# Two groups of narrow heads packed side by side before the output projections of a Flamingo-style stack

## The reference

```python
x = x + tanh(g_xattn[0]) * L0_xattn(layernorm(x), ctx)         # 16 heads of 64 over the context: "wide"
x = x + tanh(g_ffn[0])   * L0_ffn(layernorm(x))                # 16 heads of 16 over x, then 8 routed experts
x = x + tanh(g_xattn[1]) * L1_xattn(ctx, ctx, layernorm(x), mask, w_out, b_out)  # 16 heads of 16 over the context, masked
x = x + tanh(g_ffn[1])   * L1_ffn(layernorm(x))                # 16 heads of 16 over x, plus a dense mixture of 8 experts
```

## Time and profile before

| | |
|---|---|
| median of 3 runs | 3478.32 us (3477.23 to 3482.04) |
| profiled execution, its own time | 3479.19 us |
| its span, first to last instruction | 3477.0 us |
| TensorE busy | 3308.9 us (95%) |
| VectorE busy | 2020.1 us (58%) |
| ScalarE busy | 1439.3 us (41%) |
| GpSimd busy | 957.2 us (28%) |
| mean granted TensorE clock | 0.978 of full speed |

### The profile page before, as it was taken

How to read it: one execution, slowest core, us unless ns; L and a number is a source line. 1 busy time by engine, 2 the same in 40 slices (tenths; PEclk the granted TensorE clock), 3 DMA queues, 4 the chain that set the end, 5 groups by cost and what they waited for, 6 DMA issues and landing times.

```text
span 3477.0 us, 45530 instructions
## 1 busy us (share of the span) xinstructions
PE 3308.9 (95%) x18530; PEld 1442.0 (41%) x18530; DVE 2020.1 (58%) x4314; ACT 1439.3 (41%) x1645; POOL 957.2 (28%) x469
## 2 busy tenths in 40 slices
PE   7999999999999999999997979998999999999999
PEld 4444444444444445434442752223323343333354
DVE  4444445554665465565565027776767677666546
ACT  3443434444334443344433212454454435544434
POOL 4665555454465553554500000110000000000000
PEclk9999999999999999999999999999999999999999
DMA  4000000000000000000021430211111111110000
GB/s 154 11 13 13 32 8 11 13 7 32 8 19 11 13 26 8 25 10 8 4 97 49 125 108 18 60 39 49 35 35 36 35 29 25 51 35 26 13 19 13
DMA packets 68252, 114.94 MB, mean 33 GB/s; under 512 B 4849, under 2 KB 49545, under 8 KB 67530
## 3 DMA queue, kind: packets, MB, share of 16 engines
q1 hardware_dynamic: 62666, 97.08, 8.8%
q0 software_dynamic: 5376, 14.95, 1.9%
HBM read 101.79 MB, written 16.78 MB: 34 GB/s over the span
## 4 chain that ended last, share of the span: by engine, by line
PE 85%; DVE 7%; ACT 4%; POOL 2%; DMA 1%; issue 1%; ACTq 0%; DVEq 0%; POOLq 0%
PE ring L1266 10%; PE pv L1160 10%; PE ring L1149 9%; PE pv L1287 9%; PE ring L1227 3%; PE ring L1259 3%; PE ring L1121 3%; PE ring L1130 3%; PE ring L1122 3%; PE ring L1146 3%; PE ring L1107 3%; PE ring L1272 2%; PE ring L1108 2%; ACT wide L1435 2%; PE ring L1345 2%; PE ring L1326 2%
## 5 line engine op out<-in xcount | busy, mean ns | idle before, releaser
L1532 POOL TENSOR_TENSOR wide<-wide 124x1024 f32<-124x1024 f32 (+1 forms) x341 | 804.2, 2358 | 263.9 <-ACT wide L1428 227.7
L1435 ACT ACTIVATE wide<-ring 124x1024 f32<-124x1024 f32 (+2 forms) x544 | 528.5, 1022 | 549.4 <-PE ring L1266 547.0
L1651 DVE TENSOR_REDUCE max_a<-ring 128x2 f32<-128x802 f32 x512 | 491.9, 991 | 373.0 <-PE ring L1130 372.8
L1428 ACT ACTIVATE wide<-ring 124x1024 f32<-124x1024 f32 (+1 forms) x416 | 425.6, 1027 | 445.5 <-PE ring L1149 404.3
L1679 DVE CUSTOM_DVE_ANT_0 rest<-ring,slim 128x401 bf16<-128x401 f32 x683 | 374.3, 577 | 138.1 <-PE ring L1227 134.2
L1149 PE MATMUL ring<-wide 64*124 64x512 f32 (+1 forms) x1664 | 428.6, 593 | 0.0
L1160 PE MATMUL pv<-wide 124*64 124x512 f32 (+1 forms) x1664 | 413.0, 611 | 3.5 <-ACT wide L1428 3.5
L1689 DVE TENSOR_REDUCE slim<-ring 128x2 f32<-128x1024 f32 x256 | 307.5, 1221 | 111.6 <-PE ring L1239 110.3
L1266 PE MATMUL ring<-slim 32*128 32x512 f32 x2176 | 351.1, 646 | 3.0 <-DVE max_b L1679 2.3
L1502 POOL DMA_DIRECT2D slim<-in_ctx_k x16 | 8.8, 549 | 992.8 <-PE ring L1227 628.6
L1529 POOL TENSOR_TENSOR wide<-wide 124x1024 f32<-124x1024 f32 x31 | 73.4, 2369 | 557.9 <-ACT wide L1428 435.7
(11 more groups left out here) (239 smaller groups left out, 4096.2 us busy)
## 6 DMA issues: line engine op xcount, KB each, us to landing
slim<-in_ctx_k SPq DMA_DIRECT2D x16, 800.5 KB, 4.3
wide<-in_w_pair SPq DMA_DIRECT2D x32, 384.0 KB, 3.1
slim<-in_ctx_v SPq DMA_DIRECT2D x16, 744.0 KB
wide<-in_w SPq DMA_DIRECT2D x16, 512.0 KB, 4.8
wide<-in_we SPq DMA_DIRECT2D x16, 512.0 KB, 3.7
wide<-in_ctxT SPq DMA_DIRECT2D x4, 1601.0 KB, 6.6
slim<-in_ctx_k POOLq DMA_DIRECT2D x16, 400.2 KB, 4.7
wide<-padded_x SPq DMA_DIRECT2D x8, 640.0 KB, 4.8
```

The lines of the kernel that those rows point to most:

```text
L1428: sc.activation(exps_a[0:kn, slot_of[unit], :], slot[0:kn, :], ACT.Exp, scale=WIDE ** -0.5).then_inc(scalar_done, 1)
L1435: sc.activation((exps_2 if blk == 2 else exps_34)[0:kn, first + 2 * i:first + 2 * i + 2, :].rearrange("p h n -> p (h n)"), ring_t[0:kn, ba ...
L1532: po.tensor_tensor(sums[0:kn, :], sums[0:kn, :], view, ALU.add).then_inc(pool_done, 1)
L1651: ve.reduce_max(max_a[:, :, q, c], slot.rearrange("p (h n) -> p h n", h=2)[:, :, 0:CHUNK], AX.X).then_inc(vector_done, 1)
```

## The change

The host now packs the projection weights without padding: `ow` and `w_out` come as two tiles of 128 full rows instead of four with 64 zero rows. Rows 32h to 32h+15 of tile i belong to head h of group 2i, and rows 32h+16 to 32h+31 to head h of group 2i+1. In `tailb` the product of VectorE no longer goes back into `rest` but into one half of each block of 32 columns in a tile that two groups share (the upper half of `outT`). The transpose back is done once for two groups, behind the second. `outb` has two matmuls instead of four for each 128 tokens; in block 4 these have 128 columns each instead of 64. The wait for `outT` to be free stands ahead of the product instead of the transpose. `scatter` grows by 64 columns. The order strings are other ones, with the new costs, and the first `kproj` of a batch is kept behind the last `vproj` of the batch before.

```diff
-C_BASE = C_SCATTER + GROUP * SLIM
+C_BASE = C_SCATTER + P
...
+    def side_by_side(w, places):
+        out = w[places].reshape(GROUPS // 2, 2, GROUP, SLIM, w.shape[-1]).transpose(0, 2, 1, 3, 4)
+        return np.ascontiguousarray(out.reshape(GROUPS // 2, P, w.shape[-1]).transpose(1, 0, 2))
...
-        "ow": padded(a("L0_ffn_ow"), KV_MAJOR), "w_out": padded(a("L1_xattn_w_out").T, HEAD_MAJOR),
+        "ow": side_by_side(a("L0_ffn_ow"), KV_MAJOR), "w_out": side_by_side(a("L1_xattn_w_out").T, HEAD_MAJOR),
...
-    "33333332333333333333333233330030331103033113003130311130003113003111332233334300031333113003033113030331113000"
+    "33333332333333333333333233330030331130011330033130311130003113003111333233432300303310331113000313331130003113"
...
+    if unit[0] == "tailb":
+        v = 4 if unit[3] % 2 else 3
...
+                held = (("vproj", b - 1, PAIRS - 1, 1),) if b and p == 0 else ()
...
-            yield Step(0.88, (("sc", 0.6), ("ve", 2.3)) if last else (), 0, (("scoreb", blk, b, g, k),) + valued + also,
+            yield Step(0.88, (("sc", 0.6), ("ve", 2.25 if g % 2 else 1.55)) if last else (), 0, (("scoreb", blk, b, g, k),) + valued + also,
...
-        yield Step(7.0 if blk != 4 else 4.4, (("ve", 2.5),), 1,
+        yield Step(3.5 if blk != 4 else 2.2, (("ve", 2.5),), 1,
...
-                        for g in range(GROUPS):
+                        for i in range(GROUPS // 2):
                             if blk == 4:
-                                c0 = q * D + g * GROUP * SLIM
-                                last = pe.matmul(slot[:, c0:c0 + GROUP * SLIM], outT_b[blk][:, g, q * P:(q + 1) * P], scatter,
-                                                 start=True, stop=True)
+                                last = pe.matmul(slot[:, q * D + i * P:q * D + (i + 1) * P], outT_b[blk][:, i, q * P:(q + 1) * P],
+                                                 scatter, start=True, stop=True)
                             else:
-                                last = pe.matmul(slot[:, q * D:(q + 1) * D], outT_b[blk][:, g, q * P:(q + 1) * P],
-                                                 (w_out2 if blk == 2 else w_out3)[:, g, :], start=g == 0, stop=g == GROUPS - 1)
+                                last = pe.matmul(slot[:, q * D:(q + 1) * D], outT_b[blk][:, i, q * P:(q + 1) * P],
+                                                 (w_out2 if blk == 2 else w_out3)[:, i, :], start=i == 0, stop=i == GROUPS // 2 - 1)
...
-                    ve.tensor_tensor(blocks(rest)[:, :, 0:SLIM], blocks(rest)[:, :, 0:SLIM],
+                    for lane, other in plan.tile_free[unit]:
+                        past.wait_ge(*at(lane, *other))
+                    two, side = outT_b[blk][:, GROUPS // 2 + g // 2, :], SLIM * (g % 2)
+                    ve.tensor_tensor(blocks(two)[:, :, side:side + SLIM], blocks(rest)[:, :, 0:SLIM],
                                      inverse[:, :].unsqueeze(2).to_broadcast([P, S // 32, SLIM]), ALU.mult).then_inc(vector_done, 1)
-                    after(n + 3)
-                    for lane, other in plan.tile_free[unit]:
-                        past.wait_ge(*at(lane, *other))
-                    ve.transpose(outT_b[blk][:, g, :], rest[:, :]).then_inc(vector_done, 1)
+                    if g % 2:
+                        after(n + 3)
+                        ve.transpose(outT_b[blk][:, g // 2, :], two).then_inc(vector_done, 1)
```

More of the change, by code:

```diff
@@ L82, in lay_out @@
         consts[HEAD_MAJOR[g] % P, C_STRIP + g * P + STRIP] = 1
-    consts[STRIP - 1, C_SCATTER + np.arange(GROUP * SLIM)] = 1
+    consts[:, C_SCATTER:C_BASE] = np.eye(P).reshape(2, GROUP, SLIM, P).transpose(1, 0, 2, 3).reshape(P, P)
     consts[:, C_BASE:C_SPARE] = CAPACITY * np.arange(EXPERTS)
@@ L145 @@
[L145 to L149, removed]
@@ L158 @@
+    "111744745575755555555555555656575565576557557656575657565755765657565576575766767677777777"
 )
 TURNS_3 = (
[L162 to L165 removed]
@@ L171 @@
[L171 to L174 removed]
+    "00333333333333333333333333333333333333333331333133231303231332332011323323112013233231333231333233133331332332"
@@ L175 @@
+    "32231333254171462452171421241421421254624146521712561652175622674644746444747444474455464546454644467445546454"
+    "6454644467445546454464546447476575656576676"
 )
@@ L382, in wide_prep @@
                 for c in range(2):
-                    yield Step(2.75, (("sc", 0.9), ("ve", 0.6)), 1, gate, ("kproj", b, p, c))
+                    yield Step(2.75, (("sc", 0.9), ("ve", 0.6)), 1, gate + held, ("kproj", b, p, c))
                     emit(on(in_slot(("kproj", b, p, c), "scalar"), *k_free[s], *free["kB"]))
@@ L766, in flamingo @@
         wide = sb("wide", [P, 20736])
-        slim = sb("slim", [P, 19361])
+        slim = sb("slim", [P, 18849])
         consts = sb("consts", [P, C_ALL])
@@ L869, in flamingo @@
         gqa_w = part(slim, 12032, FT, (GROUPS + 1) * P + KV_HEADS * SLIM)
-        w_out2 = part(slim, 13440, GROUPS, D)
+        w_out2 = part(slim, 13440, GROUPS // 2, D)
         xn_a = part(slim, 14464, QT, D)
@@ L880, in flamingo @@
         kq_3b = half(slim, 14210, CTX + 1 + S)
-        w_out3 = part(slim, 15488, GROUPS, D)
-        xnT_3 = part(slim, 16512, FT, S)
-        low_b = half(slim, 18560, CTX)
+        w_out3 = part(slim, 15488, GROUPS // 2, D)
+        xnT_3 = part(slim, 16000, FT, S)
+        low_b = half(slim, 18048, CTX)
         max_junk = (rest[:, 0:S // 2].bitcast(BF16)[:, 0:CHUNK], rest[:, S // 2:S].bitcast(BF16)[:, 0:CHUNK],
                     half(slim, 15267, CHUNK))
-        neg_cols = {2: part(slim, 11520, QT, P), 3: part(slim, 17536, QT, P), 4: part(slim, 18048, QT, P)}
+        neg_cols = {2: part(slim, 11520, QT, P), 3: part(slim, 17024, QT, P), 4: part(slim, 17536, QT, P)}
         outT_b = {2: part(slim, 9472, GROUPS, S), 3: part(wide, 17664, GROUPS, S),
```

53 lines of the change are left out of this document (27 added, 26 removed).

## The result

The changed kernel takes 3419.91 us (median of 4 runs, 3415.08 to 3421.88) where the kernel beside it takes 3477.78 (3477.14 to 3482.04). The ratio is 0.9833, with a 95% interval of 0.9821 to 0.9845: faster by 57.9 us. The profiled execution took 3415.08 us, its span is 3413.1.

A forecast was written before the change was run, and what follows sets the result against it. TensorE, with records in work for 3308.9 of 3477.0 us, was taken as the bound. The terms 28.4 + 7.4 + 3.3 + 3.2 summed to 42.3 us off 3479.2: forecast 3437 us, range 3420 to 3460.

The forecast's parts named there:

- Blocks 2 and 3, 28.4 us: Eight projections of blocks 2 and 3 lose half their matmuls, 3.55 us each: 28.4 us, bounds 22 and 28.4.
- Block 4, 7.4 us: Block 4's four projections: 8 matmuls of 128 columns replace 16 of 64, cost following count: 7.4 us, bounds 0 and 7.4.
- Changes of tiling and the context load, 3.3 + 3.2 us: 33 fewer passings between array tilings on TensorE, 3.3 us; shorter waits between last `vproj` and `kproj`, 3.2 us.
- the order gives more: Rival: the 6.0 us wait vanishes and stretch 1200 to 1500 idles like its neighbour: 19 us more, 3418 us; chance 0.08.
- the wait of 6.0 us: At block 3's first projection: TensorE's wait of 3.66 us plus 2.35 us of slow-clock records, priced at 6.0 us.
- VectorE, 0: 24 of 48 transposes back go, 17 us of VectorE, beside TensorE work and so costed at nothing.
- Waits take some of it back: Rival: two to four waits of 6.0 us at thinly covered projections return 12 to 24 us: 3449 to 3461; chance 0.15.
- The thin cover: At block 3's first projection only 2.5 us of TensorE work covers a group's tail of 2.84 us.
- Slower after all: Rival: TensorE stands behind the tail at eight of twelve projections, 48 us lost, 3485 us; chance 0.03.
- columns rule in block 4: Rival: by the gap rule block 4's projections keep their 3.53 to 3.71 us, 7.4 us less gain, 3444 us; chance 0.03.
- The signs named ahead: Projections of 3.55 and 1.76 us, 24 transposes, TensorE busy some 38 us less, idle near 165 us, `kproj` waits 4.5, 0.6, 0.7.
- the two signs of being wrong: TensorE's idle time growing by more than 10 us, or the projection behind the thin cover waiting over 4 us.

The follow-up runs named there:

- the packing alone: Packed weights and tiles with the order, banks and buffers of the kernel before, against that kernel: 3456.73 us, ratio 0.9918; later 3454.77 and 3457.04 us.
- the second session: The changed kernel, unchanged, timed again beside a kernel before of 3477.84 us: 3423.04 us, ratio 0.9843.
- new first string: The change's order string for blocks 1 and 2 (TURNS_1); with the packing and the old string for blocks 3 and 4: 3425.76 us, 0.9824 against the kernel before.
- new second string: The change's order string for blocks 3 and 4 (TURNS_3); with the packing and the old string for blocks 1 and 2: 3458.99 us, 0.9922 against the kernel before.

## Why the forecast was right in direction and short in size

**Blocks 2 and 3, 28.4 us: right.** 16 records of 128x256 in 3.65 us to the end of the last, and TensorE's busy time fell by 35.3 us with the packing alone, for 28.4 + 7.4 forecast. End to end the packing is worth 30.0, 32.3 and 33.7 us in three sessions. The missing 2 to 6 us are mostly waits that the shorter projections uncover, 4.7 in the profile; the prediction put that bound at 22 for the first term and named the mechanism. One reading was wrong: TensorE is 97% busy or more in two of the three stretches shown, but 92.6% (277.8 of 300 us) in the one from 1200 us, where a projection of block 2 stands.

**Block 4, 7.4 us: right at its place.** By cutting its matmuls in two I got the old price back at each projection, so the count decides and not the columns. From start to the end of the last record the four gained 7.0 us; the sum had taken a pace from start to start (1.76) off a time to the end of the last record (3.71). The gap rule of the Trainium skill ("TensorE: Matmul & The Clock Gate", "Back-to-back issue gap") would have had this term at nothing; the trace does not agree with it for these matmuls. The same section gives that rule for a matmul by itself only, and has weight load and matmul together set the spacing in a stream; the halved matmuls are in line with that. Yet the whole kernel showed only 0.5 us of the difference.

**Changes of tiling and the context load, 3.3 + 3.2 us: the step that failed.** These two terms were all that the sum gave the order, 6.5 us, and the order was worth 26.3 and 28.6. The terms themselves were small either way. The waits at the second, third and fourth batch were forecast at 4.5, 0.6 and 0.7 us and are 4.62, 1.19 and 1.83: 7.6 us where 9.0 stood before, so 1.3 us less instead of 3.2. The 3.3 us for tilings were measured by no run. What failed is that every other wait was left as it was, at nothing: I had priced only what can be counted in the order itself. The stretch from 1200 us was in front of me with 22.2 us idle, and the waits for `max_a` came to 21.2 us in a view that I had not put into the sum; two of the three long ones stand in that stretch, at 1354 and 1485 us. Of the 21.2 us 15.8 went, other waits came and went, and in all 15.6 to 20.4 us of idle time went ahead of the gather. I had that as the rival "the order gives more", at 19 us and a chance of 0.08. It is nearest to the result: the stretch from 1200 gave 10.7 of its 13.3 us, and the wait of 6.0 us at the first projection of block 3 vanished as described. What it lacked is the rest of the first part: with fewer waits 5 to 12 us came from less low clock, and 2 to 5 from elsewhere. It also lacked the second part, where a new wait for `max_b` or, with the packing, the low clock took back what the 6.0 us had given.

**Luck.** The time came as near to the range as it did because two misses work against each other: the packing gave 2 to 6 us less than its terms, the order some 20 more. On which side of 3420 it fell is chance; with the gain of the second session, 54.8 us, it would have been 3423 us.

**VectorE, 0: right**, 1.7 us and within the noise. **Waits take some of it back: didn't come.** The thin cover cost 0.97 us. A wait of 5.4 us for `max_b` appeared elsewhere in block 3, and the packing in the old order has 4.7 us more idle time; but behind the gather the new order as a whole waits less than the old one with the packing, not more. It is the low clock there that took the gain. **Slower after all, and columns rule in block 4: didn't come.**

The signs named ahead: TensorE's busy time would be 38 us less and is 46.2 less; its idle time near 165 us, and it is 150.4. Neither of the two signs of being wrong appeared: idle time did not grow, and the projection behind the thin cover waited 0.97 us. Both looked for a loss, and the miss was on the other side. The 16 records of a projection start 223 ns apart on average at full clock, for the 222 named.

## What to carry to other kernels

Where a change removes work and finds the order anew, price the new order by the long waits of the old one, and give a good share of them a chance to go; counting passings in the order misses most of it. Read the granted clock of every run beside its time: an order can wait less and still lose, by more records at the low clock. Run the new order without the new work, and the new work in the old order, before believing either sum. And before explaining a stretch that grew in one profile, profile the unchanged kernel in the same session, and the changed one in a second session.

## What the runs showed of the hardware that I had not expected

- One program took 309.7 and 318.0 us for the same stretch in two sessions, and the kernel before 306.5 and 315.9. The longer time came both times with the same two stalls of ScalarE and VectorE, some 75 and 235 us behind the first gather. No wait in the trace explains them, and the length of the programs doesn't either. In the profiles of the kernel before they are most of the 9.4 us between two sessions.
- Less waiting comes with less low clock, but at no fixed rate: 16.0, 20.4 and 15.6 us less idle came with 27.3, 13.7 and 20.5 us less of the low clock. With the new first string the low clock was granted for 64.9 to 81.9 us ahead of the gather in nine profiles, with the old one for 88.7 to 99.0 in eleven.
- The low clock can undo a better order: with the packing, the new second string waits 4 to 5 us less and has 29 us more of its records at the low clock.
- A float32 matmul of 64 columns, each with its own weight load, costs TensorE as much as one of 128: 3.52 us for 32 records against 1.98 for 16.
